# A two-layer decoder on one core: decay exponent in one 64-row product, expert up products in fp16 passes, evacuations by an engine table

## The reference, cut to what matters

```python
x = x + L0_attn(ln(x))          # 16 heads of 8, rope, causal
x = x + L0_xattn(ln(x), ctx)    # 64 context tokens
x = x + L0_ffn(ln(x))           # norm, product, 8 fixed experts with GELU, product, GELU
x = x + L1_attn(ln(x))          # mLSTM: gates zi, zf, decay, 64 features
x = x + L1_xattn(ln(x), ctx)    # causal self attention plus cross attention
x = x + L1_ffn(ln(x))           # mixture of 8 experts, top 2
```

```python
# mLSTM, recurrent form in the reference
m_t = maximum(zf_t + m, zi_t); i_p = exp(zi_t - m_t); f_p = exp(zf_t + m - m_t)
C_t = f_p * C + i_p * (v_t outer k_t); h = o_t * (C_t q_t) / max(|n_t . q_t|, 1)
# mixture of experts; every token is computed for every expert
h = relu(einsum('td,ehd->teh', xf, w1) + b1)      # e = 8, h = 512, d = 128
expert_out = einsum('teh,edh->ted', h, w2) + b2
out = einsum('ted,te->td', expert_out, combine)   # combine is zero but for the top two
```

## Time and profile before

| | us |
|---|---|
| median of 3 runs | 396.71 |
| lowest, highest | 393.55, 396.99 |
| the profiled execution's own time | 397.64 |
| its span, first to last instruction | 395.9 |
| PE busy | 343.0 (87%) |
| DVE busy | 220.4 (56%) |
| ACT busy | 217.7 (55%) |
| POOL busy | 84.3 (21%) |
| mean granted TensorE clock | 0.922 of 2.4 GHz |

### The profile page before, as it was taken

The page is one execution under the profiler, slowest core; times in us unless marked ns, Lnnn a source line. Parts: engine busy times, 40 slices in busy tenths (PEclk is TensorE's granted clock), DMA queues, the critical chain, the costliest instruction groups (busy, mean ns, idle before and its releaser), DMA issues.

```text
span 395.9 us, 8364 instructions
## 1 busy us (share of the span) xinstructions
PE 343.0 (87%) x3048; PEld 239.5 (60%) x3048; DVE 220.4 (56%) x642; ACT 217.7 (55%) x419; POOL 84.3 (21%) x186
## 2 busy tenths in 40 slices
PE   1647998786978958787999999999999999999995
PEld 0432455453966846453556677884767888668755
DVE  3778558884366567978346687856321456122112
ACT  1348887769768464356054775445756444531440
POOL 3757877323333052300002200000000000000000
PEclk9995999999999866968567999999999999999999
DMA  7920000000000460000000000000000000000000
GB/s 207 418 88 2 2 2 2 2 2 0 2 2 1 170 256 2 0 2 0 2 2 0 2 2 2 2 0 2 3 2 15 2 0 15 0 2 0 2 1 28
DMA packets 4186, 12.31 MB, mean 31 GB/s; under 512 B 490, under 2 KB 2802, under 8 KB 3122
## 3 DMA queue, kind: packets, MB, share of 16 engines
q1 hardware_dynamic: 4146, 11.77, 8.0%
HBM read 11.24 MB, written 0.52 MB: 30 GB/s over the span
## 4 chain that ended last, share of the span: by engine, by line
PE 67%; DVE 14%; ACT 9%; issue 5%; DMA 2%; POOL 2%; SPq 1%; DVEq 0%; ACTq 0%; POOLq 0%
PE double L1599 14%; PE single L1610 12%; PE single L1272 6%; PE single L1264 5%; PE outs L1369 4%; PE double L1320 3%; DVE mx L1115 3%; PE double L1316 2%; PE double L1610 2%; ACT xn L803 2%; ACT region_p L844 2%; DVE mxc L1102 2%; DMA row<-in_row 2%; PE outs L1377 2%; PE double L1485 1%
## 5 line engine op out<-in xcount | busy, mean ns | idle before, releaser
L844 ACT ACTIVATE region_p<-double 128x1024 f32<-128x1024 f32 x64 | 64.3, 1028 | 25.6 <-PE double L1320 18.5
L918 ACT ACTIVATE hidden<-double,col 128x256 f32<-128x256 f32 (+1 forms) x96 | 45.3, 546 | 52.2 <-PE double L1599 52.2
L1599 PE MATMUL double<-xnT,w 128*128 128x256 f32 (+1 forms) x192 | 59.4, 455 | 0.0
L1244 DVE SCALAR_TENSOR_TENSOR x<-single,comb,x 128x128 f32<-128x128 f32 x54 | 15.8, 345 | 65.9 <-PE single L1610 65.8
L1610 PEld LDWEIGHTS single<-w,hidden 128*128 128x128 f32 x432 | 50.0, 192 | 2.8 <-issue 2.3
L1610 PE MATMUL single<-w,hidden 128*128 128x128 f32 x432 | 50.8, 276 | 0.0
L684 POOL TENSOR_SCALAR rstd<-mv 128x2 f32<-128x2 f32 x24 | 5.5, 228 | 209.9 <-DVE mv L979 209.3
L1599 PEld LDWEIGHTS double<-xnT,w 128*128 128x128 f32 x192 | 34.5, 190 | 16.8 <-issue 13.7
L1115 DVE TENSOR_REDUCE mx<-double 128x4 f32<-128x1024 f32 (+1 forms) x24 | 29.4, 1226 | 8.8 <-PE double L1485 8.2
L1369 PE MATMUL outs<-region_p,vst 128*32 128x256 f32 x256 | 22.4, 436 | 0.0
L1102 DVE TENSOR_REDUCE mxc<-double 128x16 f32<-128x1024 f32 x16 | 19.6, 1224 | 3.5 <-PE double L1464 3.1
(11 more groups left out here) (251 smaller groups left out, 650.4 us busy)
## 6 DMA issues: line engine op xcount, KB each, us to landing
w<-in_w1a SPq DMA_DIRECT2D x2, 1024.0 KB, 11.0
w<-in_w2a SPq DMA_DIRECT2D x2, 1024.0 KB, 12.6
w<-in_w1b SPq DMA_DIRECT2D x2, 1024.0 KB, 7.7
w<-in_w2b SPq DMA_DIRECT2D x2, 1024.0 KB, 10.5
row<-in_row SPq DMA_DIRECT2D x1, 800.0 KB, 7.4
wb<-in_wb SPq DMA_DIRECT2D x1, 709.0 KB, 8.5
x<-in_x SPq DMA_DIRECT2D x4, 128.0 KB, 2.8
out<-x SPq DMA_DIRECT2D x4, 128.0 KB, 1.9
```

What stands on the lines that cost most here:

```text
L844: a.activation(probs[:, slot("prob", key), :], psum(step), ACT.Exp, scale=SCALE).then_inc(psum_done[PSUM.slot(step)], 1)
L918: a.activation(dst[:, c, 0:w], psum(step)[:, k * w:(k + 1) * w], ACT.Relu, bias=colv("b1m", e * HC + c)).then_inc(psum_done[PSUM.slot(step ...
L1244: ins = v.scalar_tensor_tensor(x[:, t, :], psum(step)[:, i * P:(i + 1) * P], comb[:, t, e:e + 1], x[:, t, :], ALU.mult, ALU.add)
L1599: ins = mm(o if w == T else two(o), w1[:, e, c * P:(c + 1) * P], n6T, start=True, stop=True)
```

## The change

1. **Decay.** The two one-row products become one with 64 contraction rows (partitions 64 to 127): one row of each operand is ones, at different places, the rows between are zeros that GpSimd sets once (in `presets1`). The fp32 products of an `("ml", b, 0)` step go from six to four.
2. **Expert up products in fp16 passes.** Weights and inputs are each split into an fp16 high and low part; each fp32 product becomes three fp16 ones that accumulate (high x high, high x low, low x high). New steps `ws` (8, one an expert: ScalarE writes the high part, VectorE the low part, 128x1024 in fp16 in the place of the expert before; weights are scaled by 64) and `xs` (4, one a sequence: GpSimd writes high and low part of the normed input). `mup` now waits for both. Biases are scaled once; the scale is taken out in the combine weights.
3. **Engine table.** `BY_VECTOR` lists 46 steps whose ScalarE part VectorE does in its place: transposes and attention outputs of layers 0 and 1 (`tr`, `ou`, `oc`), four `lnb` of norm 2, some `tq` and `tqm`, `ml.2.2`, two `gc`, and 14 of the 32 `mup` (10 of the pair's, 4 of sequence 3's). The context's `kct` goes the other way, from VectorE to ScalarE.
4. **Order.** A new `ORDER_TABLE` of 521 steps from planner times that are 0.05 us longer for TensorE parts, 1.36 for `mup` and 0.83 for `("ml", b, 0)`; with it buffers and banks are given out anew. Around the new steps it reads: `ws` 0 to 5 between the first `mxs` of sequence 1 and the last `pv` of its self attention, `ws` 6 and 7 among the steps of sequences 0 and 2; and at the end `tr.6.2 gb.0 mdown.2.6 xs.2 mup.2.7.0 gc.0 ga.2 gb.2 mup.0.0.0`.

```diff
-BY_SCALAR = (2, 3, 4)
+SHIFTED = (2, 3, 4)
+WSCALE = 64.0
...
+BY_VECTOR = (
+    12, 28, 73, 76, 91, 93, 98, 100, 114, 138, 147, 149, 152, 153, 167, 169, 174, 190, 191, 217,
+    235, 241, 264, 284, 289, 298, 302, 328, 397, 442, 444, 451, 457, 460, 462, 463, 465, 466, 468,
+    469, 471, 472, 493, 495, 497, 503,
+)
...
     def add(step, after, *parts, behind=()):
+        if len(steps) in BY_VECTOR:
+            parts = [("D", vector_time(step)) if engine == "A" else (engine, t) for engine, t in parts]
...
-        add(("ml", b, 0), [("rows", b)], ("P", 1.43), ("A", 0.49), ("D", 0.56))
+        add(("ml", b, 0), [("rows", b)], ("P", 0.83), ("A", 0.49), ("D", 0.56))
...
-                add(("mup", g, e, q), [("tr", 6, b) for b in group], ("P", 1.71),
-                    ("A", 1.36 if n == 2 else 1.6),
+                add(("mup", g, e, q), [("xs", b) for b in group] + [("ws", e)], ("P", 1.36),
+                    ("A", 1.26 if n == 2 else 1.57),
...
+    for e in range(NE):
+        add(("ws", e), [("tr3", 0), ("tr3", 1), e and ("ws", e - 1)] + [("lnb", 1, b) for b in every] +
+            [("q1", b) for b in every], ("A", 0.63), ("D", 0.69))
+    for b in every:
+        add(("xs", b), [("tr", 6, b)], ("G", 1.15))
...
+        pair_rows, one_place = slice(DH, P), slice(96, 97)
+        row_keys = of_tmp(every, 3852 + T, 2 * T).rearrange("p (s t) -> p s t", s=2)
+        row_queries = sb("row_queries", [P, 2, T])
+        rowa, rowg = row_keys[gate_row], row_queries[one_place]
...
+        w1s = [(row[:, 0:512] if e == 0 else w1[:, e - 1, :]).bitcast(F16).rearrange(
+            "p (s n) -> p s n", s=2) for e in range(NE)]
+        xs = xnT[:, 0, :].bitcast(F16).rearrange("p (m q s t) -> p q s m t", m=2, q=2, s=2)
...
# GpSimd
+                elif kind == "xs":
+                    written(pool, ("tr", 6, b))
+                    hi, lo = (xs[:, b % 2, n, b // 2, :] for n in range(2))
+                    src = xnT[:, 1, toks(b)]
+                    then(g.tensor_copy(hi, src))
+                    then(g.tensor_tensor(lo, src, hi, ALU.subtract), "x_split")
                 elif kind == "presets1":
+                    for t, place in ((row_keys, one_place), (row_queries, gate_row)):
+                        then(g.memset(t[pair_rows, :, :], 0.0))
+                        then(g.memset(t[place, :, :], 1.0), "row_ones")
...
# ScalarE
+                elif kind == "ws":
+                    e = step[1]
...
+                        act.wait_ge(sem("w_split"), e)
+                    then(a.activation(w1s[e][:, 0, :], w1[:, e, :], ACT.Copy, scale=WSCALE), "w_high")
...
# VectorE
+                elif kind == "ws":
+                    e = step[1]
+                    dve.wait_ge(sem("w_high"), e + 1)
+                    then(v.scalar_tensor_tensor(w1s[e][:, 1, :], w1[:, e, :], WSCALE, w1s[e][:, 0, :],
+                                                ALU.mult, ALU.subtract), "w_split", wait=False)
...
+                elif kind == "mup" and by_vector(step):
...
+                        v.tensor_scalar(dst[:, c, 0:w], psum(step)[:, k * w:(k + 1) * w],
+                                        b1s[:, e * HC + c:e * HC + c + 1], 0.0,
+                                        ALU.add, ALU.max).then_inc(
+                            psum_done[PSUM.slot(step)], 1)
...
# TensorE
-                        mm(o, rowa[:, w, kt * P:(kt + 1) * P], one_row[:, 0:n], start=True, stop=False)
-                        mm(o, one_row[:, 0:P], rowg[:, w, ts], start=False, stop=False)
+                        mm(o, row_keys[pair_rows, w, kt * P:(kt + 1) * P],
+                           row_queries[pair_rows, w, ts], start=True, stop=False)
...
-                        written(pe, ("tr", 6, b))
-                    pe.wait_ge(sem(f"w1b_loaded{e // 4}"), 16)
+                        pe.wait_ge(sem("x_split"), count(("xs",), ("xs", b)))
+                    pe.wait_ge(sem("w_split"), e + 1)
...
-                        ins = mm(o if w == T else two(o), w1[:, e, c * P:(c + 1) * P], n6T,
-                                 start=True, stop=True)
+                        for m, (w_part, x_part) in enumerate(((0, 0), (0, 1), (1, 0))):
+                            ins = mm(o if w == T else two(o), w1s[e][:, w_part, c * P:(c + 1) * P],
+                                     xs[:, b, x_part] if w > T else xs[:, b % 2, x_part, b // 2, :],
+                                     start=m == 0, stop=m == 2)
```

More of the change, by code:

```diff
@@ L150, with vector_time @@
           "nxa": "gelu"}
+VECTOR = {"tr": 0.35, "tr2": 0.75, "tr3": 0.37, "ou": 0.35, "ml": 0.35, "tq": 0.7, "tqm": 0.7, "tk4": 0.7,
+          "kct": 0.7, "oc": 0.6, "gc": 0.41, "mup": 1.2}
+BY_VECTOR = (
[3 more added lines that the diff above has]
+)
+def vector_time(step):
+    if step[0] == "lnb":
+        return {2: 1.13, 3: 1.13, 4: 0.62}.get(step[1])
+    if step[0] == "ml" and step[2] != 2:
+        return None
+    if step[0] == "mup" and len(GROUPS[step[1]]) == 1:
+        return 1.45
+    return VECTOR.get(step[0])
 def the_steps():
@@ L477, in decoder @@
         b2m = sb("b2m", [NE, P])
+        b1s = sb("b1s", [P, NE * HC])
         w1 = sb("w1", [P, NE, HC * P])
@@ L611, in normed @@
         def normed(eng, s, b):
-            n = sum(1 for t in ORDER[:INDEX["lnb", s, b] + 1]
-                    if t[0] == "lnb" and (t[1] in BY_SCALAR) == (s in BY_SCALAR))
-            eng.wait_ge(sem("xn_by_scalar" if s in BY_SCALAR else "xn_ready"), n)
+            mine = by_vector(("lnb", s, b))
+            n = sum(1 for t in ORDER[:INDEX["lnb", s, b] + 1] if t[0] == "lnb" and by_vector(t) == mine)
+            eng.wait_ge(sem("xn_by_vector" if mine else "xn_by_scalar"), n)
         def biased(step):
@@ L737, in _ @@
                 elif kind == "presets0":
-                    then(g.memset(one_row, 1.0))
                     then(g.memset(vst[:, :, :, :], 0.0))
@@ L795, in _ @@
                 kind, b = step[0], step[-1]
-                if kind == "lnb" and step[1] in BY_SCALAR:
+                if by_vector(step):
+                    continue
+                if kind == "lnb":
                     s = step[1]
@@ L828, in _ @@
                          psum16(step)[:, 0:640].rearrange("p (g t) -> p g t", g=5))
+                elif kind == "kct":
+                    if b == 4:
+                        for n in range(NB):
+                            act.wait_ge(psum_full, PSUM.full(("sc", 1, n, 1)))
+                    stack_evac(step, kcT)
                 elif kind in ("tq", "tqm"):
@@ L965, in key_stack, with evac, stack_evac @@
                 then(v.tensor_copy(q[:, :, 8:16], q[:, :, 0:8]), "stack_ready")
+            def evac(key, out_ap, in_ap, scale=None):
+                dve.wait_ge(psum_full, PSUM.full(key))
+                gives(key, v.tensor_copy(out_ap, in_ap) if scale is None else
+                      v.tensor_scalar(out_ap, in_ap, scale, None, ALU.mult))
+            def stack_evac(step, dst):
+                evac(step, dst[:, :, :].rearrange("p g (i t) -> p i g t", i=2),
+                     psum16(step).rearrange("p (i g t) -> p i g t", i=2, g=4))
             for step in ORDER:
@@ L979, in _ @@
                     then(v.bn_aggr(mv[:, h, t1, :], stat[:, h, t1, :]), "var_ready")
-                elif kind == "lnb" and step[1] not in BY_SCALAR:
+                elif kind == "lnb" and by_vector(step):
                     s = step[1]
```

179 lines of the change are left out of this document (114 added, 65 removed), and 53 rows, old and new, of the table ORDER_TABLE.

## The result

| | before | after |
|---|---|---|
| median of 4 runs, us | 396.85 | 375.20 |
| lowest, highest | 393.55, 398.84 | 373.65, 376.02 |
| profiled execution, span | 397.64, 395.9 | 373.65, 371.9 |
| PE, DVE, ACT, POOL busy | 343.0, 220.4, 217.7, 84.3 | 314.7, 268.1, 186.5, 92.0 |
| mean granted clock | 0.922 | 0.963 |

The ratio is 0.9458 (95% interval 0.9385 to 0.953): some 21 us or 5.4% less. The forecast was 378 us (366 to 389). Executions of one kernel differ by up to 3%, with other granted clocks; medians here are over all of them, ratios leave the slow ones out.

The account below looks back on a forecast made before the run. TensorE was taken to bound the kernel behind 186 us, with ScalarE, TensorE and VectorE taking turns ahead of it. 397.6 - 13.7 - 3.2 + 0.5 + 2.5 - 5 + 2 - 2 = 378.7, so median 378 us, range 366 to 389.

Parts of the forecast that it names:

- Up products: Expert up products behind 228 us: three 16-bit passes save 0.43 us a step over 32 steps, 13.7 us in all.
- handoffs: Waits between TensorE and the engines evacuating the faster up products, over the whole mixture: 2 us lost, bounds 0 and 8.
- Weight loads: Loads of 128x128 16-bit weights in the up-product steps, taken to cost nothing; bounds 0 to 104 ns each.
- Rival C: In all 32 up-product steps each 16-bit pass pays for its weight load: slower, 408.7 us; chance 0.03.
- Decay columns: In the decay of all four sequences, 384 fp32 columns fewer per sequence save 3.2 us in all.
- Clock: TensorE's granted clock, low from 186 to 228 us: 2 us gained, between 13.5 gained and 13 lost.
- rival B: The clock stays at 2.4 GHz through most of 186 to 228 us: 10 us more gained, 368 us; chance 0.16.
- Engine table and order ahead of 186 us: Evacuations moved from ScalarE to VectorE and the new order gain 5 us together; bounds 3 lost and 10 gained.
- `ws`: Splitting the expert weights costs 2.5 us where VectorE holds the chain, 155 to 186 us; bounds 0 and 4.5.
- Memsets: GpSimd's four new memsets in the first 30 us cost 0.5 us, at most 1.7.
- `xs`: GpSimd's splitting of the inputs stays hidden behind TensorE work: cost 0, up to 1.5 us without that cover.
- Rival A: VectorE becomes the bound from 155 to 262 us and near the end: 385 us, at most 391.7; chance 0.14.

Follow-up runs that it names:

- run 4: The changed kernel with the mixture's up products in fp32 again and no splitting of weights and inputs, order and engine table kept: 384.41 us, ratio 0.9614.
- run 9: The changed kernel with the first pair up-product step of experts 3 to 6 evacuated by ScalarE, the second by VectorE: 374.29 us beside the changed kernel's 373.98.
- run 3: The changed kernel with an extra 64-row product ahead of each decay product, which overwrites it: 377.14 us.
- run 2: The changed kernel with an extra one-row product ahead of each decay product, which overwrites it: 388.14 us.
- run 6: The kernel before, in its order and engines, with the 64-row decay product alone: median 391.25 us, between 382.73 and 393.77 in ten executions.
- run 5: The kernel before, in its order and engines, with the 64-row decay product and the fp16 up products put in: 379.55 us, ratio 0.951.
- runs 1: The changed kernel with its decay exponent again as two one-row products, all else kept: 388.58 us, ratio 0.9732.

## Why the prediction was right, point by point

The main mechanism held: TensorE bounds the second part, and what it saves there is saved. One term, the clock, was wrong by a factor of about four. Term by term, with the caution that what is read off one profile carries that execution's clock:

- *Up products,* -13.7 with +2 for handoffs: measured 11.2 us behind the first exponential (run 4's profile) and 9.2 to 10.4 between medians. A step of 1.30 us was right (1.31). The handoffs took 2.3 us and not 2, on the chain's count all among the pair's steps; the forecast wanted to avoid them by alternating the engines, but run 9 does just that and gains nothing: with two wide banks filling and evacuation stay in the way.
- *Weight loads,* 0: right. They are recorded with 98 ns each, and twelve of them, 1.18 us, lie inside a step of 1.31 us whose passes alone need 1.28. Rival C falls. The rule of the Trainium skill that it drew on ("TensorE: Matmul & The Clock Gate", section "Part 3": a weight load overlaps running matmuls only if it goes to other rows) does not agree with this trace: all 128 rows are in use, and the loads overlap.
- *Decay columns,* -3.2: the 64-row extra product costs 1.9 us over the changed kernel's first median and 3.2 over its second (run 3): right within what the medians tell.
- *Clock,* -2, "near nothing, as the 32-row work around it stays": this is the step that failed. The columns aside, one-row products cost 11 us (run 2 less run 3: 388.14 - 377.14), and behind the first exponential, with up products and columns taken out of the 21.5 us, 8 to 9 are left for the clock. The 32-row scores and 32-column values stayed and ran at full clock. It is rival B's mechanism, and its sign, a mean clock over 0.96, was there with 0.963. By the Trainium skill ("TensorE: Matmul & The Clock Gate", section "Why this matters for your kernels") a continuously busy TensorE goes to the full clock. These traces do not agree that being busy is enough: the one-row form is busy 6.00 of 6.00 us from 210 to 216 us at a clock of 0.50.
- *Engine table and order ahead of 186 us,* -5, and *`ws`,* +2.5: neither term was measured as sized, their sum was nearer. The first exponential comes at 184.2 us in the kernel before and at 182.2 with the decay product alone (run 6), so 2.0 us are the decay's. Without splitting, new order and table come there at 182.0 (run 4), no earlier than the old ones. With splitting they come at 181.7, the old order at 187.1 (run 5). So what order and table give ahead of 186 us is room for `ws`, which costs nothing in the new order and up to 4.9 us in the old one, part of it clock. The instruction takes VectorE 0.69 us, estimated at 0.8.
- *Memsets,* +0.5: not separated.
- *`xs`:* hidden, as said: TensorE never waits for it.

Rival A did not come: from 186 us on VectorE is at 84% and 89% (35.2 of 42 and 30.2 of 34 us), yet TensorE stays full (40.5 of 42, 33.9 of 34). From 155 to 186 us VectorE is at 95% and TensorE, as before, at three quarters. VectorE's busy time rose by 47.7 us and ScalarE's fell by 31.2, both as forecast. That the total came out 3 us from the forecast is in part luck. The clock gave 6 to 7 us more than its 2. Against that, ahead of the first exponential 2.5 us came where the terms add to 3.3, and up products and columns behind it gave about 1 less; the two profiles differ by 24.0 us against 18.9 forecast. And the two profiled executions lie 24.0 us apart where the medians lie 21.6, which took another 2 off the miss.

The three parts do not add up one by one. In the changed kernel undoing the decay costs 13.4 us; alone in the kernel before it brought some 8 in its shortest executions. The clock is the likely reason: the same product decides about a stretch of 20 us or not, depending on what stands around it (runs 1 and 6).

## What to carry to other kernels

Where TensorE is full and its granted clock still low, look for matmuls with one row in that stretch and fill their rows, even with zeros: the same columns cost the same (0.67 us here either way), and the clock may stay up for everything around them. It need not: in run 6 it did not. An fp32 product as three fp16 passes saves its quarter of streaming in full (1.73 to 1.31 us a step here), if the split hides elsewhere, but in a run of steps what it saves is capped by the number of banks: a step can't take less than filling plus evacuation plus handoffs, over the banks (2.99 / 2 us here). An order laid out for an engine table can't be judged without it, nor the table without the order; swap both.

## What the runs showed of the hardware that was not expected

- Two products alike in columns, place and recorded time (0.67 us), one with 1 row and one with 64, of which all but two rows are zeros: with the first TensorE's granted clock falls to 0.50 in the same step and the kernel takes 388.1 us, with the second it stays at 1.00 there and the kernel takes 377.1.
- In the 6 us ahead of that fall TensorE is busy 5.38 of 6.00 us in both forms, so busy time does not tell them apart. From 210 to 216 us of the one-row form the clock is 0.50 with TensorE busy 6.00 of 6.00 us: a low granted clock does not need an idle gap.
- The clock differs between executions of one kernel too: the decay product alone in the old order ran between 382.7 and 393.8 us, with mean granted clocks of 0.926 to 0.963.
- Twelve loads of 128x128 fp16 weights, recorded with 98 ns each, and the twelve passes of 256 columns that use them take 1.31 us together, with all 128 rows in use.
